# Keys of the last attention normed and turned in the mixing stage; one stream of the row mixing on ScalarE

## What is computed

```python
H_res = sinkhorn_log(H_res_logits)              # 50 iterations
H_res = (1.0 - g) * I + g * H_res
x_mixed = jnp.einsum('btij,btjc->btic', H_res, x_streams)
y_distributed = jnp.einsum('btc,btn->btnc', y, H_post)
return (x_mixed + y_distributed).reshape(B, T, nC)
```

```python
k = (cross_attention_states @ Wk.T)...          # 8 groups, 128 features each
k = _rmsnorm(k, k_norm_w)                       # x * rsqrt(mean(x*x) + 1e-5) * w
scores = jnp.einsum('bhqd,bhkd->bhqk', q, k) * scale
```

## Time and profile before

| | us |
|---|---|
| median of 3 runs | 1451.11 (1449.87 to 1452.61) |
| the profiled execution, its own time | 1449.24 |
| its span, first to last instruction | 1446.8 |
| mean granted clock of PE | 0.994 |

### The profile page before, as it was taken

One profiled execution on the slowest core, in us unless ns is written; L12 is line 12 of the kernel. 1 busy time (PEld: TensorE's weight loads), 2 busy tenths in 40 slices (PEclk: granted clock), 3 DMA queues, 4 the chain that ended last, 5 costly groups with the idle time before them and its releaser, 6 DMA issues.

```text
span 1446.8 us, 24538 instructions
## 1 busy us (share of the span) xinstructions
PE 1401.5 (97%) x7713; PEld 1175.1 (81%) x7713; DVE 1065.7 (74%) x2471; ACT 872.1 (60%) x2194; POOL 590.3 (41%) x631
## 2 busy tenths in 40 slices
PE   8999999999999999999999999999999999999997
PEld 7888888887788767778788788777888888888875
DVE  5697667687787876766775775768788788778885
ACT  5556555555423456755756755658777677677661
POOL 3555444444122146555655645335133243242121
PEclk9999999999999999999999999999999999999999
DMA  8011110112123240331331221320111012012000
GB/s 327 1 74 73 74 58 14 73 34 103 59 88 131 80 155 30 131 102 37 125 102 68 92 102 59 130 87 17 54 49 74 16 74 87 15 73 80 1 1 30
DMA packets 30135, 107.75 MB, mean 74 GB/s; under 512 B 3847, under 2 KB 13191, under 8 KB 22104
## 3 DMA queue, kind: packets, MB, share of 16 engines
q1 hardware_dynamic: 30040, 106.58, 20.3%
HBM read 97.07 MB, written 9.50 MB: 74 GB/s over the span
## 4 chain that ended last, share of the span: by engine, by line
PE 65%; DVE 15%; issue 8%; ACT 6%; POOL 5%; DMA 0%; POOLq 0%; DVEq 0%; ACTq 0%; SPq 0%
PE bank L192 14%; PE bank L193 14%; PE bank L194 14%; PE bank L1979 3%; POOL wq_low L1249 2%; PE bank L341 2%; PE bank L1994 2%; PE bank L364 2%; PE bank L2000 2%; PE bank L1996 2%; PE bank L310 2%; PE bank L1937 1%; PE bank L352 1%; DVE logit L2291 1%; DVE p_low L2309 1%
## 5 line engine op out<-in xcount | busy, mean ns | idle before, releaser
L165 POOL TENSOR_TENSOR tmp<-tmp,sin 128x512 f32<-128x512 f32 x80 | 106.6, 1332 | 218.1 <-ACT tmp L150 216.2
L194 PE MATMUL bank<-wo_low,att_high 128*128 128x512 f32 x384 | 150.6, 392 | 0.0
L2291 DVE SCALAR_TENSOR_TENSOR logit<-bank,qss,amask 128x512 f32<-128x512 f32 x128 | 91.1, 748 | 57.1 <-PE bank L194 56.0
L2197 POOL TENSOR_TENSOR qss<-qss,half 128x4 f32<-128x4 f32 x32 | 34.9, 1090 | 198.7 <-DVE qss L2277 198.7
L1808 PE MATMUL bank<-kT,wg 128*128 128x256 f32 x512 | 112.2, 380 | 3.6 <-ACT prob L1843 3.6
L2098 ACT ACTIVATE prob<-logit,rmax 128x512 f32<-128x512 f32 x128 | 91.6, 719 | 38.4 <-DVE rmax L2295 38.4
L1808 PEld LDWEIGHTS bank<-kT,wg 128*128 128x128 f32 x512 | 96.7, 190 | 17.8 <-ACT prob L1843 4.7
L149 ACT ACTIVATE tmp<-bank 64x512 f32<-64x512 f32 x80 | 47.6, 595 | 104.3 <-PE bank L194 98.3
L192 PE MATMUL bank<-l_wo_high,att_high 128*128 128x512 f32 x256 | 104.6, 408 | 1.8 <-DVE att_low L1692 1.1
L193 PE MATMUL bank<-xT_high,wq_low 128*128 128x512 f32 x256 | 102.1, 399 | 0.0
L193 PE MATMUL bank<-l_wo_high,att_low 128*128 128x512 f32 x256 | 99.8, 390 | 0.0
(11 more groups left out here) (323 smaller groups left out, 4394.5 us busy)
## 6 DMA issues: line engine op xcount, KB each, us to landing
wq<-in_l_wq SPq DMA_DIRECT2D x16, 1024.0 KB, 5.5
wo<-in_l_wo SPq DMA_DIRECT2D x16, 1024.0 KB, 4.9
wkv<-in_l_wkv SPq DMA_DIRECT2D x16, 512.0 KB, 5.6
wg<-in_l_wg SPq DMA_DIRECT2D x8, 1024.0 KB, 4.8
wq<-in_x_wq SPq DMA_DIRECT2D x8, 1024.0 KB, 7.1
wo<-in_x_wo SPq DMA_DIRECT2D x8, 1024.0 KB, 4.9
kT<-in_x_wkv SPq DMA_DIRECT2D x8, 512.0 KB, 4.2
kv_keys<-logit SPq DMA_DIRECT2D x8, 512.0 KB, 4.5
```

The source lines that it names most:

```text
L165: eng.tensor_tensor(halves(tmp[4 + j % 2]), halves(tmp[2 + j % 2]), per_batch(sin), ALU.mult).then_inc(sem(f"{l}_sinp"), 1)
L194: return eng.matmul(dst, a_high, b_low, start=False, stop=stop)
L2291: dve.scalar_tensor_tensor(logit[s % 2][:, c, :], bank[3 + c][:, :], qss[p][:, 1, h, 2 * b + c:2 * b + c + 1], amask[:, c, :], ALU.mult, A ...
```

## The change

Each projected unit's keys are squared and summed by ACT in the mixing stage. For each half group (2 units) ACT forms the norm by Ln and Exp (`kv_key_rms`), scales the rows, PE turns them (`kv_turn_keys`) into one of two banks, and ACT copies them back over the rows (`kv_keys_out`); SP stores the turned keys. The last attention loads them turned and makes its high and low parts from SBUF; its squares, mean, power, product and transposes are gone. In the row mixing ACT now makes stream 0 alone, for tiles 1 to 3; DVE makes the rest. The windows become 4, 4, 5, 4, 13.

```diff
+                dve.memset(key_eps, 1e-5)
...
-        mixed = [[tmp[t][:, :] for t in range(NT)], [xT[:, t, :] for t in range(NT)]]
+        mixed = [tmp[t][:, :] for t in range(NT)]
...
-            if t == 0:
+            if t == 1:
...
-            for j in range(2):
-                for i in range(STREAMS):
-                    last = act.activation(mixed[j][t][:, i * P:(i + 1) * P], x[:, t, j * P:(j + 1) * P], ACT.Copy,
-                                          scale=hres[:, t, i * 4 + j:i * 4 + j + 1])
+            for i in range(STREAMS):
+                last = act.activation(mixed[t][:, i * P:(i + 1) * P], x[:, t, 0:P], ACT.Copy,
+                                      scale=hres[:, t, i * 4:i * 4 + 1])
...
-                for j in (2, 3):
+                for j in range(1 if t else 0, STREAMS):
...
-                        dve.wait_ge(sem("branch_part"), 2 * NT + t + 1)
-                        for part in mixed:
-                            step(dve, dve.tensor_tensor(acc[:, :], acc[:, :], part[t], ALU.add))
-                        at = [tally[0]] * STREAMS
+                        if t:
+                            dve.wait_ge(sem("branch_part"), 2 * NT + t)
+                            step(dve, dve.tensor_tensor(acc[:, :], acc[:, :], mixed[t], ALU.add))
+                            at = [tally[0]] * STREAMS
...
-                    if i == 4 and k in (5, 6):
-                        mix_streams(act, 2 * (k - 5))
-                        mix_streams(act, 2 * (k - 5) + 1)
+                    if i == 4 and k in (6, 7, 8):
+                        mix_streams(act, k - 5)
+                    if unit == 3:
+                        kv_key_rms(act, 0)
+                    if unit % 2 == 0 and unit < 4 * NG:
+                        kv_key_rms(act, unit // 2 - 1)
+                    if unit == 4:
+                        kv_keys_out(act, 0)
+                    if unit % 2 == 1 and unit >= 5:
+                        kv_keys_out(act, unit // 2 - 1)
...
-        KV_WINDOWS = [3, 5, 5, 6, 11]
+        KV_WINDOWS = [4, 4, 5, 4, 13]
+        KEY_BANKS = [0, 3]
...
-                sp.wait_ge(sem("kv_copied"), 4 * g + 4)
-                for dst, src in (("kv_keys", logit), ("kv_values", prob)):
+                for dst, src, done, per in (("kv_values", prob, "kv_copied", 4), ("kv_keys", logit, "kv_keyT", 2)):
+                    sp.wait_ge(sem(done), per * g + per)
...
+                    if isinstance(g, int) and g == 0:
+                        if n == 3:
+                            kv_turn_keys(pe, 0, 0, 0)
+                    elif n % 2 == 0:
+                        kv_turn_keys(pe, 2 * g - 1 + n // 2, *((1 - p, 4) if n == 0 else (p, 0)))
...
+        def kv_turn_keys(pe, half_, p, at):
+
+            pe.wait_ge(sem("kv_rms"), 6 if isinstance(half_, int) and half_ == 0 else 5 * half_ + 5)
+            if due(half_ - 1):
+                pe.wait_ge(sem("kv_keyT"), half_ - 1)
+            for t in range(4):
+                last = pe.transpose(bank[KEY_BANKS[at // 4]][:, t * P:(t + 1) * P],
+                                    flat(logit[p])[:, (at + t) * P:(at + t + 1) * P], ident[:, :])
+            last.then_inc(sem("kv_turn"), 1)
...
+            for i in range(2):
+                last = act.activation(ysq[:, n // 2, (2 * n + i) % 4 * HD:(2 * n + i) % 4 * HD + HD], src[:, i, 0:HD], ACT.Square,
+                                      accum_out=kss[:, 0, 2 * n + i:2 * n + i + 1])
+            last.then_inc(sem("kv_rms"), 1)
...
+        def kv_key_rms(act, half_):
+
+            tiles = slice(half_ % 2 * 4, half_ % 2 * 4 + 4)
+            act.wait_ge(sem("kv_rms"), rms_squares(half_))
+            act.activation(kss[:, 1, tiles], kss[:, 0, tiles], ACT.Ln, bias=key_eps, scale=1.0 / HD)\
+               .then_inc(sem("kv_rms"), 1)
+            act.wait_ge(sem("kv_rms"), rms_squares(half_) + 1)
+            act.activation(kss[:, 2, tiles], kss[:, 1, tiles], ACT.Exp, scale=-0.5).then_inc(sem("kv_rms"), 1)
+            act.wait_ge(sem("kv_rms"), rms_squares(half_) + 2)
+            act.wait_ge(sem("kv_copied"), 2 * half_ + 2)
+            for t in range(half_ % 2 * 4, half_ % 2 * 4 + 4):
+                rows_ = flat(logit[half_ // 2 % 2])[:, t * P:(t + 1) * P]
+                last = act.activation(rows_, rows_, ACT.Copy, scale=kss[:, 2, t:t + 1])
+            last.then_inc(sem("kv_rms"), 1)
+
+        def kv_keys_out(act, half_):
+
+            act.wait_ge(sem("kv_turn"), half_ + 1)
+            act.activation(flat(logit[half_ // 2 % 2])[:, half_ % 2 * 512:half_ % 2 * 512 + 512],
+                           bank[KEY_BANKS[half_ % 2]][:, :], ACT.Copy).then_inc(sem("kv_keyT"), 1)
...
-                act.wait_ge(sem("x_kturn"), 2 * m + half_ + 1)
-                act.activation(k_high[p][:, half_ * C:(half_ + 1) * C], bank[5 + half_][:, :], ACT.Copy,
+                act.activation(k_high[p][:, half_ * C:(half_ + 1) * C], raw_keys(p, half_)[:, :], ACT.Copy,
...
-                        if s == 6 and half_ == 0 and not last_group:
-                            pe.wait_ge(sem("x_klow"), 2 * n + 1)
-                        if s == -1 and half_ == 1:
-                            pe.wait_ge(sem("x_klow"), 2 * g + 2)
...
-                        if not last_group:
-                            turn_keys(n, 1 - p, s - 6, 16 * g + 2 * (s - 1) + s - 5)
...
-            for k in range(2):
-                ln_scalar(act, 2, k)
+            ln_scalar(act, 2, 0)
+            kv_key_rms(act, 2 * NG - 1)
+            ln_scalar(act, 2, 1)
+            kv_keys_out(act, 2 * NG - 1)
...
-            keep_busy(pe, 14, bank[1])
+            keep_busy(pe, 6, bank[1])
             pe.wait_ge(sem("kv_copied"), 4 * NG)
             ln_tensor(pe, 2, 1)
-            keep_busy(pe, 6, bank[1])
+            kv_turn_keys(pe, 2 * NG - 1, 1, 4)
+            keep_busy(pe, 3, bank[1])
```

More of the change, by code:

```diff
@@ L1845, in kv_copy, with rms_squares @@
             last.then_inc(sem("kv_copied"), 1)
+        key_eps = yss[0][:, 0, 0:1]
+        def rms_squares(half_):
+            return 3 if half_ == 0 else 5 * half_ + 2
+        def kv_key_rms(act, half_):
[15 more added lines that the diff above has]
+                           bank[KEY_BANKS[half_ % 2]][:, :], ACT.Copy).then_inc(sem("kv_keyT"), 1)
         xT_low = over("xT_low", [P, KC, T], "xT")
@@ L1939, in query_sums @@
                 last.then_inc(sem("x_qss"), 1)
-            def turn_keys(m, p, half_, turned):
-                pe.wait_ge(sem("x_kn"), 2 * m + half_ + 1)
-                if turned is not None:
-                    pe.wait_ge(sem("x_plow"), turned)
-                for t in range(4):
-                    last = pe.transpose(bank[5 + half_][:, t * P:(t + 1) * P],
-                                        raw_keys(p, half_)[:, t * P:(t + 1) * P], ident[:, :])
-                last.then_inc(sem("x_kturn"), 1)
             def body(g, p, last_group):
@@ L2053, in x_tensor @@
                 query(0, 0, h, None)
-            for half_ in range(2):
-                turn_keys(0, 0, half_, None)
             for h in range(2):
@@ L2058, in x_tensor @@
             piped_groups(nc.tensor, body)
-        def x_squares(act, m, p, half_):
-            if half_ == 0:
-                act.wait_ge(sem(f"x_keys{p}"), 16 * (m - p) + 32)
-            for t in range(half_ * CT, (half_ + 1) * CT):
-                last = act.activation(ysq[:, half_, t % CT * P:(t % CT + 1) * P],
-                                      raw_keys(p, half_)[:, t % CT * P:(t % CT + 1) * P], ACT.Square,
-                                      accum_out=kss[:, 0, t:t + 1])
-            last.then_inc(sem("x_ksq"), 1)
         def x_scalar(act):
@@ L2084, in keys_out @@
             def keys_out(m, p, half_):
-                act.wait_ge(sem("x_kturn"), 2 * m + half_ + 1)
-                act.activation(k_high[p][:, half_ * C:(half_ + 1) * C], bank[5 + half_][:, :], ACT.Copy,
+                if half_ == 0:
+                    act.wait_ge(sem(f"x_keys{p}"), 16 * (m - p) + 32)
+                    if due(16 * (m - 1)):
+                        act.wait_ge(sem("x_score"), 16 * (m - 1))
+                act.activation(k_high[p][:, half_ * C:(half_ + 1) * C], raw_keys(p, half_)[:, :], ACT.Copy,
                                scale=dvec[:, 3:4]).then_inc(sem("x_k"), 1)
@@ L2186, in x_gpsimd_first @@
             low_weights(pool, "split", wq_high[0], wq_low[0], wq[0])
-        def x_key_pow(pool, m):
-            pool.wait_ge(sem("x_kmean"), m + 1)
-            mean, rms = (kss[:, k, :].rearrange("p (b t) -> p b t", b=B) for k in (1, 2))
-            pool.tensor_tensor(rms, mean, half[:, :].unsqueeze(1).broadcast_to([P, B, CT]), ALU.pow)\
-                .then_inc(sem("x_krms"), 1)
         def x_gpsimd(pool):
@@ L2264, in keys_rest @@
                 at = (slice(None), slice(half_ * C, (half_ + 1) * C))
-                dve.scalar_tensor_tensor(k_low[p][at], bank[5 + half_][:, :], dvec[:, 3:4],
```

(13 more changed lines are left out.)

17 lines of the change are left out of this document (1 added, 16 removed).

## The result

The changed kernel takes 1463.01 us in the median of 4 runs (1462.44 to 1465.47), the kernel before, run beside it, 1451.57: a ratio of 1.0083, with a 95% interval of 1.0071 to 1.0096. The forecast was 1456.7 with a range of 1448.5 to 1460.5: slower, as said, but by twice as much, and outside the range. The profiled execution has a span of 1460.2 us against 1446.8, 13.4 more; the forecast had 5.6. The 10.9 that are left fit the 11.4 of the medians.

A forecast was written before the change was run, and what follows sets the result against it. The prediction took PE to bound both the mixing stage and the last attention. Mixing and dt +15.1 (0.2 + 6.9 + 5.0 - 1.2 + 2.7 + 1.5) less 9.5 gave +5.6 us: 1451.11 becomes 1456.7, range 1448.5 to 1460.5.

The forecast's parts named there:

- Last attention, what goes: Last attention: removed transpose blocks -6.3, probabilities' transposes no longer waiting -2.2, group 0 -1.0; sum -9.5 us.
- may also do less: Last attention: if probabilities' transposes wait for something besides the keys' banks, 3 us of 9.5 stay away, 1459.7; no separate chance.
- slower still: Mixing stage: the norm takes 2.5 us, not 1.7, so blocks wait longer and closings slip: +5 more, 1462; chance 0.09.
- New waits: Mixing stage: PE waits for ACT sum to 8.6 us against 3.6 before, +5.0.
- clock: Mixing stage: one more fall of PE's clock to half speed, expected after (d): +1.5 us (0 to 3).
- (a): Mixing stage: block 0 of PE's key transposes waits 0.5 us for the first norm.
- (e): Mixing stage: transpose blocks 12 and 13 wait 0.7 us each behind a stream of the mixing on ACT.
- (b): Mixing stage: PE's branch sums wait 2.4 us for ACT's fourth branch scaling, queued behind window 0's closing and other work.
- (c): Mixing stage: transpose block 7 waits 1.2 us, since ACT copies unit 15 only after the closing of window 2.
- (d): Mixing stage: transpose block 9 waits 3.2 us, since ACT copies and norms unit 19 only after window 3 closes.
- No change: Whole kernel: only half the waits come (short ones vanish or norm is faster), no clock fall: about 0, 1451; chance 0.25.
- faster: Mixing stage: PE takes no waits for ACT and no clock fall follows: -4.5 us, 1446.6; chance 0.13.

The follow-up runs named there:

- fill_keys_first: Changed kernel with ACT taking high keys before query weights in last-attention steps 6 and 7, plus four idle PE transposes in each of those steps: 1462.53 us, ratio 1.0075.
- fill_after: Changed kernel plus four idle PE transposes in steps 6 and 7 of each last-attention group but the last: 1467.61 us, ratio 1.0109.
- before_keys_first: Kernel before the change, with ACT taking the high keys ahead of the query weights in last-attention steps 6 and 7: 1448.39 us, ratio 0.9982.
- before_one_stream: Kernel before the change with only the row mixing changed (one stream on ACT, rest on DVE), keys untouched: 1450.88 us, ratio 1.0000.
- old_rows: Changed kernel with the row mixing undone, two streams back on ACT for all four tiles: 1469.73 us, ratio 1.013.
- late_windows: Changed kernel with mixing-stage transpose blocks and ACT's copies out one unit later, and windows 4, 4, 5, 5, 12: 1456.22 us, ratio 1.004.

## Why the prediction was wrong

**"Last attention, what goes": -9.5, measured 0.** This is the step that failed, by more than the whole miss of the span, 7.8 us. Term by term:
- "A block costs 0.45 us of PE; 14 of the 16 blocks lie in full groups: -6.3." The price was right: where the ring is out of the way, `fill_keys_first` pays 0.9 us for two blocks. But steps 6, 7 and 0 take 7.40 + 6.49 + 7.61 = 21.50 us of PE without them, and the 7.61 has 1.11 of new wait in it. That the blocks lie on the path was wrong for twelve of the fourteen. They lay in steps 6 and 7, in the shadow of the ring; `fill_after` shows 0.2 us a group for two blocks. The forecast's "at least -6.3" took for granted that PE's work is the path. The two of group 6, where there is no ring, gave the 0.9 us by which the last stretch is shorter.
- "The transposes of the probabilities no longer wait for the keys' low part: -2.2." These waits went, and were no price of the keys' banks: they were where the ring came to the surface. Six waits, in groups 0 to 5, and none in group 6, already said so; the prediction read the name of the releaser, and not what DVE had been waiting for itself (ACT's high keys, 1.88 us).
- "Group 0: -1.0." The wait for the high probabilities fell from 1.07 to 0.40, but it is 0.40 as well in two of the three other traces with the old keys (`before_keys_first`, `before_one_stream`), so it can't be booked as the change's. From amask to the next group's mark it took 1.7 us longer, with a fall of the clock (0.61 from 994 to 998) behind a wait of 1.88 that the kernel before has too, there without a fall. This stretch takes 117.3 to 119.8 us in the four traces with the old keys and 117.0 to 120.1 in the five with the new ones, ACT's old order and no blocks put back, so the 1.7 can't be laid to the change. With the 1.0 of the steady groups and the 0.9 of the last stretch it makes the nothing of the whole; without it the stage would have given some 2.
- The rival "may also do less" had the right kind of cause, that something else stands behind the banks, but priced it at 3 us of 9.5, as an appendix, without looking for it. The number nearest to 1463.0 is that of "slower still", 1462, and that is luck: a norm takes 1.8 us (452.94 to 454.73 in ACT's timeline), near the 1.70 of the forecast and not the rival's 2.5.
- "ACT's other squares, DVE's two products and POOL's power give nothing, since PE is never idle there": true of the time, but it hid the question. In steps 6 and 7 neither DVE nor ACT lost any work, and these were the ones that counted.

**Mixing and dt: +15.1, measured 13.6**, of which 0.8 stand at 168 us already; that leaves 12.8. By parts:
- Start +0.2: the units start 0.9 late (393.46 against 392.58); less the 0.8 this is 0.1.
- Blocks +6.9: 15 x 0.44 = 6.6, right. The Trainium skill (TensorE: Matmul & The Clock Gate, Part 4: PE-mode transpose) gives some 275 ns for one 128x128 bf16 transpose within a kernel. The trace does not bear that out as a cost: four f32 ones add 0.44 us here, 110 ns each.
- New waits +5.0 (8.6 against 3.6; the five items add up to 8.7), and clock +1.5: waits of 5.35 and a fall of the clock of 1.7 came, 7.0 against 3.6, +3.5 for the two terms' 6.5. (a) 0.5 came as 0.57 and (e) 0.7 twice as 0.70 and 0.77. (b) 2.4 didn't come: ACT's fourth scaling of the branches ends at 418.7 (417.53 + 1.16), which is where the walk had it, 2.4 behind the start of the sums at 416.29. But only the last quarter of the 32 products needs it (PE waits for one scaling per tile), and PE gets there at about 419.0, three quarters into the 3.57 us between the starts of the sums and of the next unit. (c) 1.2 was 2.10. (d) 3.2 was 1.21 here, behind the fall of the clock, and 2.90 in `fill_after` without it; its size was right.
- The clock's fall had the size that was said and cost nothing, since it came behind (c) and not behind (d) and so shortened the wait at (d). In `fill_after` it came behind (d), as forecast, and cost 1.7; in `old_rows` it came behind neither.
- Last unit at 516.3, a sum that leaves the 1.5 of the clock out; with it, it would be 517.8. Measured: 515.34. Tail -1.2: dt starts 5.2 behind the unit and not 6.2, -1.1, though with a wait of 1.56 in it.
- Queue of loads +2.7, with l_wg issued at 522.3 and ACT waiting some 4 us: 521.26 and 3.94; PE resumes 543.13 - 529.25 = 13.9 late, against 10.1 at dt, so +3.8.

The sum of this half is 2.3 us too high: (b) and the clock were too high by 3.9 together, (c) and the load too low by 0.9 and 1.1. That it came out so near is in part these errors against each other. The mechanisms stood, but for the wait at (b): waits by ACT's order, a wait of SP in front of a load, no work of DVE on the path (its rows end at 510.7, PE's units at 515.3).

**"No change" and "faster".** "Faster" asked for a sum of waits under 3 us, and it was 5.35, or 7.0 with the clock. "No change" asked for the short waits (a), (c) and (e) to vanish; all of them came, and it was (b) that did not. Both took the gain of 9.5 in the last attention for granted.

## What to carry to other kernels

Ahead of taking work away from a saturated engine, ask in each step whether it is that engine's work or a ring of the others that sets the period, by subtracting the starts of one instruction in two successive steps on each engine; an engine busy for 99.7% of a stretch can be filling time that another owns, and a short wait at one place, absent in the one group that lacks some work, is the tip of such a ring. Work moved to an engine with room is paid by where it stands in that engine's list: ahead of a blocking wait it costs what the wait lasts, and the room on the mean says nothing. Behind a late store, everything in the same queue is late.

## What the hardware showed beside this

The clock of PE differs between executions of code that is the same, and the runs don't say why: the 32 products of the branches took 3.82 us in the changed kernel and 6.54 in `late_windows`, ahead of anything that differs between them, and the wait of 1.88 us in group 0 was followed by a fall in one execution (0.61) and by none in another (1.00). A single profiled execution can be 2 us off in each such place. And a fall need not cost its time: behind the wait of 2.10 us PE only waited less in the next place (17.80 against 17.82 us). The stretch behind that wait, in the changed kernel

```profile
994.00:998.00 4.00, 3.78 (x20) 3.78 (x21) 2.32 (x7) 3.32 (x8) 1.56 (x2) 0.61 0.00 0
```

and in `late_windows`:

```profile
988.00:992.00 4.00, 3.57 (x25) 3.37 (x26) 2.67 (x8) 3.33 (x8) 1.36 (x2) 1.00 0.02 4
```

The keys' low part, read from SBUF (`tmp`) instead of PSUM, takes 0.75 us as before, but 1.05 in the first of the two halves in groups with query weights, with two subtractions of POOL on query weights beside it (3.01 us from 1194.78). The second half, with such a pair beside it as well (3.00 from 1202.76), takes 0.75, so what makes the difference stays open.
